# Shared-expert input kept as high and low halves, gate products in fp32r, first products of a tile ahead of its second ones, and one routed-slot step moved from ACT to DVE

## The reference

```python
mod = silu(c) @ wmod                         # six rows of 512 per sequence: sa, ca, ga, sb, cb, gb
h = layernorm(x) * (1 + ca) + sa
qkv = rms(h) @ w_qkv.T; ...                  # cumulative sums along the tokens give y
h1 = h + (y @ w_u.T) * silu(y @ w_g.T) @ w_out.T
x = x + ga * h1
h = layernorm(x) * (1 + cb) + sb
logits = h @ gate_w                          # 8 experts, the best 2, softmax over the 2
routed = sum of gate * (gelu(h @ w1[e] + b1[e]) @ w2[e] + b2[e])
shared = gelu(h @ shared_w1 + shared_b1) @ shared_w2 + shared_b2
out = x + gb * (h + routed + shared terms)   # residual and gain as in the code
```

## Time and profile before

| | |
|---|---|
| time of 3 runs | 1948.55 us median (1946.94 to 1948.81) |
| profiled execution | 1945.63 us, its span 1943.8 us |
| PE busy | 1901.7 us of the span (98%) |
| DVE busy | 1266.5 us (65%) |
| ACT busy | 706.3 us (36%) |
| POOL busy | 277.5 us (14%) |
| DMA | 189.97 MB, mean 98 GB/s |

### The profile page before, as it was taken

How to read it: one execution, slowest core, us unless ns; L and a number is a source line. 1 busy time by engine, 2 the same in 40 slices (tenths; PEclk the granted TensorE clock), 3 DMA queues, 4 the chain that set the end, 5 groups by cost and what they waited for, 6 DMA issues and landing times.

```text
span 1943.8 us, 26200 instructions
## 1 busy us (share of the span) xinstructions
PE 1901.7 (98%) x8850; PEld 1529.6 (79%) x8850; DVE 1266.5 (65%) x2636; ACT 706.3 (36%) x1412; POOL 277.5 (14%) x251
## 2 busy tenths in 40 slices
PE   7999999999999999999999999999999999899998
PEld 4688888878888888888887787787786777688886
DVE  6789899875545554565347447457457675588887
ACT  4677776621111111123112222222233343355554
POOL 0000000000000000000001011011020220377774
PEclk9999999999999999999999999999999999999999
DMA  5313112421110111024011321311243663578886
GB/s 189 134 55 103 52 45 66 131 98 44 66 65 10 66 65 65 2 96 173 22 65 61 94 67 67 109 67 61 93 110 141 201 201 139 184 142 154 153 153 97
DMA packets 86687, 189.97 MB, mean 98 GB/s; under 512 B 9525, under 2 KB 26198, under 8 KB 81516
## 3 DMA queue, kind: packets, MB, share of 16 engines
q1 hardware_dynamic: 62988, 127.77, 19.6%
q0 software_dynamic: 23568, 60.51, 14.4%
HBM read 118.56 MB, written 72.12 MB: 98 GB/s over the span
## 4 chain that ended last, share of the span: by engine, by line
PE 88%; DVE 5%; issue 3%; POOL 2%; DMA 1%; ACT 1%; POOLq 0%; SPq 0%; DVEq 0%; ACTq 0%
PE bank L654 12%; PE bank L656 12%; PE bank L655 12%; PE bank L659 12%; PE bank L661 11%; PE bank L660 11%; PE bank L897 3%; POOL out L618 1%; PE bank L824 1%; PE bank L673 1%; PE bank L899 1%; PE bank L927 1%; PE bank L926 1%; PE bank L925 1%; PE bank L884 1%
## 5 line engine op out<-in xcount | busy, mean ns | idle before, releaser
L654 PE MATMUL bank<-x_hi,w_blk 128*128 128x512 f32 x1024 | 403.3, 394 | 4.1 <-DVE s_t L1585 3.1
L656 PE MATMUL bank<-x_hi,w_blk 128*128 128x512 f32 x1024 | 399.4, 390 | 0.0
L655 PE MATMUL bank<-x_lo,w_blk 128*128 128x512 f32 x1024 | 399.2, 390 | 0.0
L1585 DVE TENSOR_TENSOR s_t<-act_t,bank 128x512 f32<-128x512 f32 x128 | 87.9, 687 | 304.5 <-PE bank L656 304.3
L1185 ACT ACTIVATE s_hi<-s_t 128x512 fp32r<-128x512 f32 x128 | 80.9, 632 | 436.3 <-DVE s_t L1585 436.3
L654 PEld LDWEIGHTS bank<-x_hi,w_blk 128*128 128x128 f32 x1024 | 192.6, 188 | 43.7 <-DVE w_blk L1381 2.7
L656 PEld LDWEIGHTS bank<-x_hi,w_blk 128*128 128x128 f32 x1024 | 192.7, 188 | 40.8
L655 PEld LDWEIGHTS bank<-x_lo,w_blk 128*128 128x128 f32 x1024 | 192.8, 188 | 38.9
L1183 ACT ACTIVATE act_t<-bank 128x512 f32<-128x512 f32 x128 | 76.3, 596 | 347.4 <-PE bank L656 347.4
L659 PE MATMUL bank<-w_blk,s_hi 128*128 128x512 f32 x512 | 200.7, 392 | 0.0
L661 PE MATMUL bank<-w_blk,s_lo 128*128 128x512 f32 x512 | 199.4, 389 | 0.0
(11 more groups left out here) (267 smaller groups left out, 3475.3 us busy)
## 6 DMA issues: line engine op xcount, KB each, us to landing
x_t<-y_scratch SPq DMA_DIRECT2D x24, 1024.0 KB, 5.0
residual<-r_t SPq DMA_DIRECT2D x16, 1024.0 KB, 4.4
r_t<-residual SPq DMA_DIRECT2D x16, 1024.0 KB, 5.7
raw<-w_swi POOLq DMA_DIRECT2D x16, 768.0 KB, 4.5
y_scratch<-y_t SPq DMA_DIRECT2D x32, 256.0 KB, 2.7
r_t<-x_tok SPq DMA_DIRECT2D x8, 1024.0 KB, 5.3
h_rows<-hrow SPq DMA_DIRECT2D x32, 256.0 KB, 3.1
y_scratch<-hT SPq DMA_DIRECT2D x8, 1024.0 KB, 3.9
```

Of the source, the lines that this page charges most:

```text
L654: nc.tensor.matmul(dst, w[:, 0, col:col + P], rhs_hi, start=start, stop=False)
L655: nc.tensor.matmul(dst, w[:, 0, col:col + P], rhs_lo, start=False, stop=False)
L656: return nc.tensor.matmul(dst, w[:, 1, col:col + P], rhs_hi, start=False, stop=stop)
L1585: nc.vector.tensor_tensor(s_t[:, s % 2, :], act_t[:, s % 2, :], bank[4 + (2 * s + 1) % 3][:, :], ALU.mult).then_inc(f.s_ok, 1)
```

## The change

It does the following.

- The second norm's columns are kept in fp32r halves. `hT` becomes [P, chunk, 2, token]; ACT's `take_hT` writes the high part, a new DVE step `hT_lo` reads the same bank and writes the low part. PE's `rows_to_hT` for the next group, and `logits`, now wait for the low part (`hl_ok`). In pass "c", `hT_lo` stands ahead of blocks 5 to 7 and after block 7; for LAST it stands after block 3 of shared tile 0 (g = 0, 1) and after blocks 0 and 1 of tile 1 (g = 2, 3).
- SP stores both parts in two halves of 1 MB (chunks 0-1 and 2-3), and pass "s" loads such halves into three buffers `xs` (`load_half`); `up1` multiplies from them. The splits of pass "s" on ACT and DVE go. Half 3 (chunks 2-3 of tile 1) uses the buffer of half 0.
- `logits` becomes 8 fp32r matmuls of 512 columns with 16 and 8 stationary columns in place of 4 float32 ones; `logits_to_tokens` becomes 4 float32 matmuls with a small 0/1 matrix `both` that adds the two row groups, in place of 4 transposes.
- In stage 5, ACT's `slot_o` goes; DVE multiplies bank, gate and `gb_row` in one step. ACT's two weight pieces go ahead of `slot_x` in the same turn. The buffers of `o_t` are reordered, so that DVE's wait for the output moves from slot 0 to slot 1.
- In a shared tile, PE's order is up 0, 1, 2, 3, then down 0, 1, 2, 3. The hooks keep their step numbers.
- Row 0 of wmod comes in four transfers of 256 KB, and the first `modulate` waits for each quarter.
- Four small constant tables are loaded by POOL after the last list instead of before pass "c"; DVE waits for this and for the last output of the gates before it uses their memory.

The diff, cut to its core:

```diff
@@ sync
-            load_wmod(0)
+            for m in range(NC):
+                sp.dma_start(wmod_t[0][:, m * D:(m + 1) * D], wmod[MOD_ORDER[0]][:, m * D:(m + 1) * D]).then_inc(first_in[m], 16)
...
             def hT_out(u):
-                sp.wait_ge(n2.hT_ok, NSUB * (u + 1))
-                sp.dma_start(y_dram[u], hT[:, :]).then_inc(hT_st, 16)
+                sp.wait_ge(n2.hl_ok, NSUB * (u + 1))
+                for k in range(2):
+                    sp.dma_start(xs_dram[u, k], hT[:, 2 * k:2 * k + 2, :, :].bitcast(F32)).then_inc(hT_st, 16)
+            def half_left(h):
+                if h % 2 == 0:
+                    sp.wait_ge(xs_free, h // 2 + 1)
+                else:
+                    sp.wait_ge(ffn["s"].up, NB_S * (h // 2 + 1))
+            def load_half(h):
+                k, n = half_at(h)
+                if h == 0:
+                    sp.wait_ge(xl_ok, NC * NT * 2)
+                elif h < 3:
+                    sp.wait_ge(ffn["c"].up, 2 * NB * NT)
+                else:
+                    half_left(h - 3 if h < 2 * NT - 1 else h - 2)
+                sp.wait_ge(hT_st, 32 * (h // 2 + 1))
+                sp.dma_start(xs[k][:, :, :, :].bitcast(F32), xs_dram[h // 2, h % 2]).then_inc(xs_in[k], 16)
...
-                if t + 2 < NT:
-                    next_x("s", t + 2)
+                if t < LAST:
+                    if t > 0:
+                        load_half(2 * t + 2)
+                    load_half(2 * t + 3)
@@ tensor
             def rows_to_hT(u, g):
                 pe.wait_ge(n2.h_ok, NSUB * u + g + 1)
                 if NSUB * u + g > 0:
-                    pe.wait_ge(n2.hT_ok, NSUB * u + g)
+                    pe.wait_ge(n2.hl_ok, NSUB * u + g)
...
                 for m in range(NC):
-                    ins = nc.tensor.matmul(norm_bank(u)[0:E, :], gw_t[:, m * E:(m + 1) * E], ch(hT, m),
-                                           start=(m == 0), stop=(m == NC - 1))
+                    nc.tensor.matmul(norm_bank(u)[0:2 * E, :], gw2[:, m, :], hT[:, m, 0, :], start=(m == 0), stop=False)
+                    ins = nc.tensor.matmul(norm_bank(u)[0:E, :], gw2[:, m, 0:E], hT[:, m, 1, :], start=False,
+                                           stop=(m == NC - 1))
...
             def slot_down(j, at_e):
-                    pe.wait_ge(rt.og_ok, j - 1)
+                    pe.wait_ge(rt.o_ok, j - 1)
...
             def shared_tile(t):
-                    if s >= 2:
-                        down("s", t, s - 2, w_shr[:, s - 2, :, :], QKV_W, NB_S)
+                    for d in {3: (0, 1), 4: (2,), 5: (3,)}.get(s, ()):
+                        down("s", t, d, w_shr[:, d, :, :], QKV_W, NB_S)
@@ scalar
-            def split_s(t):
-                act.wait_ge(ffn["s"].up, NB_S * t)
-                split(x_in, 16 * (2 * NT + t + 1))
...
-            def slot_o(j):
...
             for j in range(NSLOT):
+                if j in R_TURNS:
+                    piece_hi(R0 + 14 + R_TURNS.index(j))
                 if j + 3 < NSLOT:
                     slot_x(j + 3)
...
-                slot_o(j)
-                if j in R_TURNS:
-                    piece_hi(R0 + 14 + R_TURNS.index(j))
@@ vector
+            def hT_lo(u, g):
+                dve.wait_ge(n2.hT_ok, NSUB * u + g + 1)
+                nc.vector.tensor_tensor(in_hT(1, g), by_chunks(norm_bank(u)), in_hT(0, g).bitcast(F32),
+                                        ALU.subtract).then_inc(n2.hl_ok, 1)
...
                     block_s(t, s)
+                    if (t, s) in ((1, 0), (1, 1)):
+                        hT_lo(LAST, 2 + s)
...
-                if t + 1 < NT:
-                    split(NC * (NT * PASS["s"] + t + 1))
+                if t == 0:
+                    hT_lo(LAST, 0)
+                    hT_lo(LAST, 1)
...
-                dve.wait_ge(rt.og_ok, j + 1)
-                if j == 0:
+                dve.wait_ge(rt.dn, j + 1)
+                if j == 1:
                     dve.wait_ge(out_st, 16 * NT)
...
-                nc.vector.tensor_tensor(o_t[j % NO][:, :], p_t[j % 2][:, :], gb_row[:, :],
-                                        ALU.mult).then_inc(rt.o_ok, 1)
+                nc.vector.scalar_tensor_tensor(out=o_t[j % NO][:, :], in0=bank_o[j % 2][:, :], scalar=gate_t[:, j:j + 1],
+                                               in1=gb_row[:, :], op0=ALU.mult, op1=ALU.mult).then_inc(rt.o_ok, 1)
```

More of the change, by code:

```diff
@@ L1847, in _ @@
                             piece_lo(i)
-                    split(NC * (NT * PASS[p] + t + 1))
+                    if p == "c" and t >= 1:
+                        hT_lo(t - 1, 3)
+                    if (p, t) != ("c", LAST):
+                        split(NC * (NT * PASS[p] + t + 1))
                     evacuate(p, t)
```

117 lines of the change are left out of this document (75 added, 42 removed).

## The result

| | before | changed |
|---|---|---|
| median of 20 runs | 1946.88 us (1943.95 to 1948.81) | 1943.22 us (1937.87 to 1946.82) |
| ratio | | 0.9977, 95% interval 0.997 to 0.9984 |
| profiled execution's span | 1943.8 us | 1941.6 us |
| PE busy | 1901.7 us | 1896.8 us |

The change gains 0.23% where 0.6% was forecast: 4 us, not 12. The time lies in the range, but two terms of the sum were wrong. The runs also spread by 9 us where those of before spread by 5. Why they spread more, no run shows.

A forecast was written before the change was run, and what follows sets the result against it. PE, busy 98% of the span, was taken as the bound. Terms -13.7 + 2.4 + 5.8 - 7.6 - 0.4 + 1.6 = -11.9 from 1948.55 gave 1936.6 us, range 1930.0 to 1945.0.

The forecast's parts named there:

- Logits, -13.7: Gate products of 8 tiles: eight fp32r matmuls at 0.227 us replace four float32 ones (3.53 us), saving 1.72 each time.
- rival 3: Gate products no faster, each at 0.43 us: 13 of the 13.7 go, +1.1, 1949.7 us; chance 0.07.
- Logits to tokens, +2.4: Four float32 products replacing four transposes take 0.34 us more, seven times; bounds 0 and +3.5.
- Shared tile 1, +5.8: PE waits 8 us for half 3 behind the residual, and the fallen clock costs 1.7; bounds +3.7 and +7.8.
- Tiles 2 to 7, 0: Shared tiles: the 3 MB of loads land 21 to 23 us into a tile, wanted at 24.8, so hidden.
- rival 2: Halves land late in shared tiles 2 to 7, each start waiting 1 to 2 us: +9, 1945.6 us; chance 0.12.
- rival 4: Still later halves in six shared tiles, each losing 2.5 us waiting and 1.7 of clock: +13.3, 1961.9 us; chance 0.05.
- The start, +1.6: Kernel start: quarters of row 0 gain only 0.1 us, while idle PE lets the clock fall; bounds -0.1 and +2.5.
- Routed start, -7.6: First routed slots: DVE's output wait moves to slot 1 and ACT's step goes, removing PE waits; bounds -4 and -9.
- End, -0.4: Kernel end: the last product goes straight from bank to `o_t` without ACT, saving 0.4 us.
- The new order, 0: PE's order in the shared tile: same work of 8 blocks, next to nothing to win in tiles 2 to 7, 0 in tile 0.

The follow-up runs named there:

- half3_early: The changed kernel with the load of half 3 moved in SP's queue ahead of the last tile's second norm and residual; 1942.04 us, ratio to before 0.9976.

## Why the prediction was wrong in two terms

- *Logits, -13.7.* Right in kind; measured some -1.9 for each of eight, -15. The 0.43 of a bias product was no guide, and rival 3 is excluded. By the Trainium skill (TensorE: Matmul & The Clock Gate, weight-path perf modes) fast weight loading needs 128 weights and an input that is not FP32; for fp32r it says nothing. Here products with 8 and 16 weights ran at 0.231 us where full ones take 0.227, so whatever their load costs is hidden.
- *Logits to tokens, +2.4.* Mis-sized. "A float32 product is recorded twice, so 0.34 more" gave 0.68; they take 0.98, +0.64 each, +4.5 for seven. Together with the logits the two errors cancel: -9.9 measured to tile 0, -10.0 reckoned. A further 0.6 came unforeseen, an idle of 0.78 at 1268 us in the kernel before, of which 0.15 is left.
- *Shared tile 1, +5.8.* Right in mechanism and nearly in size: the wait of 7.75 for a reckoned 8, and +6.8 without the logits. That `hT_lo` stands close behind, "done near 1507.2, not later", was right as well, and is why half3_early gave almost nothing.
- *Tiles 2 to 7, 0.* This step failed. "One MB alone took 4.3, one beside another 7.4; three together 11 to 13" took the landing from a stretch in which POOL wrote no list. Beside list 6 half 7 took 18.1 (12.5 to 18.1 over the kernels that don't hold it), landed 30.5 us after tile 2's start where 21 to 23 were reckoned, and tile 3 lost 4.4. It was the mechanism of rival 2 in one tile, or in the next (tile 4 in five of the experiments), not in all six, and with the clock's loss of rival 4. Not tried: why the collision falls on tile 3 in some kernels and on tile 4 in others; the two lists' times against the loads' differ by a microsecond or two between them.
- *The start, +1.6.* This step failed in its first half. The fall of the clock was foreseen and came (about 2 of 4.9). The sum left the landings where they were; "only -0.1 can come of it" bounded the gain and not the loss. The four issues are SP's and were not counted against what stands behind them in its queue, and the x rows and `raw_q` came 2.6 later, which is the larger half. Three more issues of 0.45 are 1.4 of it; the rest is a longer landing (8.6 for 7.4 before) that stays unexplained. By the Trainium skill (DMA: Bandwidth & Descriptors, anatomy) a transfer issued by GpSimd has about 2.0 us fixed; these are SP's, and the prediction used that figure for them. The runs don't show a sum of fixed parts: the quarters land 4.1 us from their issue, side by side.
- *Routed start, -7.6.* -7.7 measured, though from slot 4 to slot 8 there are four slots of 3.45 and not the "five" of the text. *End, -0.4:* nothing gained, +0.5. POOL's last write starts 2.6 us behind PE's last matmul in both, since its last three stand 2 us apart, and the time from its start to the end of the kernel is 7.5 us instead of 7.0.
- *The new order, 0.* Right.

The two failed terms, +3.3 and +4.4, are most of the difference between the -11.9 reckoned and the -2.2 between the profiled executions.
